# The dense layer of a tile group in the round of its own items, ten groups instead of nine, and a bias of three bf16 rows

## The reference

```python
neigh_sum = segment_sum(ln(x)[src], dst, num_segments=6250)      # 100000 edges, sorted by dst
deg = segment_sum(ones, dst, num_segments=6250)
h = concatenate([ln(x), neigh_sum / maximum(deg, 1.0)[:, None]], axis=-1)
out = relu(h @ W + b)                                            # 512 -> 256
x = x + out / maximum(norm(out, axis=-1), 1e-12)
gate_scores = ln(x) @ Wg.T + bg                                  # 8 experts, top 2 of each node
...
```

## Time and profile before

| what | us |
|---|---|
| median of three runs (lowest, highest) | 3768.05 (3767.71, 3769.46) |
| profiled execution: its time, and its span | 3773.36, 3771.6 |
| mean granted TensorE clock | 0.869 |
| TensorE, VectorE, ScalarE, GpSimd busy | 2839.5, 1832.5, 963.7, 1716.8 |
| gather stage of layer 0: first indirect load | 104.5 |
| last indirect load, end of the stage | 1107.9, 1263.7 |

### The profile page before, as it was taken

One profiled execution on the slowest core, in us unless ns is written; L12 is line 12 of the kernel. 1 busy time (PEld: TensorE's weight loads), 2 busy tenths in 40 slices (PEclk: granted clock), 3 DMA queues, 4 the chain that ended last, 5 costly groups with the idle time before them and its releaser, 6 DMA issues. The chain is left out here.

```text
span 3771.6 us, 56373 instructions
## 1 busy us (share of the span) xinstructions
PE 2839.5 (75%) x13227; PEld 2325.9 (62%) x13228; DVE 1832.5 (49%) x4097; ACT 963.7 (26%) x3408; POOL 1716.8 (46%) x1811
## 2 busy tenths in 40 slices
PE   1566778778877599999998536767667667738999
PEld 0355657656655388888887425555555455538998
DVE  5322333444566411111111847878788888773444
ACT  0000100100111122222222323433344344315544
POOL 0677777777740122222222067667666666300000
PEclk9888988889887699999999768888888888857999
DMA  5333333333320121222221633333333333200000
GB/s 171 92 104 105 105 104 115 114 104 111 115 73 15 68 84 57 107 70 94 85 81 31 195 110 107 98 100 104 101 101 101 101 99 98 59 17 7 21 19 21
DMA packets 152075, 326.67 MB, mean 87 GB/s; under 512 B 38677, under 2 KB 89837, under 8 KB 147870
## 3 DMA queue, kind: packets, MB, share of 16 engines
q0 software_dynamic: 85824, 236.38, 22.0%
q1 hardware_dynamic: 59758, 83.04, 6.6%
q10 hardware_dynamic: 6416, 6.42, 0.5%
HBM read 286.41 MB, written 41.40 MB: 87 GB/s over the span
## 5 line engine op out<-in xcount | busy, mean ns | idle before, releaser
L633 POOL DMA_INDIRECT G<-g_rows,srcT x784 | 745.2, 951 | 435.2 <-issue 243.3
L633 POOL DMA_INDIRECT G<-h_rows,srcT x784 | 747.4, 953 | 270.2 <-issue 236.6
L814 PE MATMUL pS<-G,O 128*128 x2336 | 593.1, 418 | 208.4 <-SPq L801 182.5
L814 PEld LDWEIGHTS pS<-G,O 128*128 128x128 f32 x2336 | 487.6, 211 | 312.1 <-issue 228.6
L1713 PE MATMUL pS<-G,O 128*128 x2336 | 637.4, 436 | 56.3 <-DVE O L1861 56.3
L1713 PEld LDWEIGHTS pS<-G,O 128*128 128x128 f32 x2336 | 491.6, 214 | 195.4 <-issue 79.7
L1341 PE MATMUL pH<-XT,w1s 128*128 128x256 f32 x1728 | 384.6, 381 | 1.4 <-SPq L1312 1.4
L1351 PE MATMUL pY<-w2s,HE 128*128 128x256 f32 x1728 | 381.9, 379 | 0.0
L1341 PEld LDWEIGHTS pH<-XT,w1s 128*128 128x128 f32 x1728 | 330.2, 191 | 47.2 <-issue 1.8
L1366 ACT ACTIVATE HE<-pH,b1s 128x256 f32<-128x256 f32 x432 | 204.9, 474 | 584.1 <-PE pH L1341 584.1
L1351 PEld LDWEIGHTS pY<-w2s,HE 128*128 128x128 f32 x1728 | 324.1, 190 | 41.8
(11 more groups left out here) (294 smaller groups left out, 3526.9 us busy)
## 6 DMA issues: line engine op xcount, KB each, us to landing
w1s<-in_W_dram SPq DMA_DIRECT2D x16, 1024.0 KB, 5.0
w2s<-in_W_dram SPq DMA_DIRECT2D x16, 1024.0 KB, 7.6
G<-h_rows,srcT POOLq DMA_INDIRECT x784, 2.8
Y<-y_rows SPq DMA_DIRECT2D x49, 256.0 KB, 4.4
G<-g_rows,srcT POOLq DMA_INDIRECT x784, 2.8
g_rows<-OUT SPq DMA_DIRECT2D x49, 132.0 KB, 2.3
h_rows<-ACC SPq DMA_DIRECT2D x7, 896.0 KB, 5.4
X<-in_x_dram SPq DMA_DIRECT2D x1, 6144.0 KB
```

The lines of the kernel that those rows point to most:

```text
L633: pool.indirect_dma_start(out=G[:, c % (ring * Q), 0:width], out_offset=None, in_=rows, in_offset=bass.IndirectOffsetOnAxis(ap=srcT[:, c:c ...
L814: mm = nc.tensor.matmul(pS[k][:, 0:W], O[:, k, q, :], G[:, bass.ds((s % R0) * Q + q, 1), :].rearrange("p a d -> p (a d)"), start=(q == 0), ...
```

## The change

1. Group r's dense layer runs in round r, right behind its items, instead of in round r + 1. All the other steps of a group move up by one round too (LAGS = 3).
2. The groups are (7, 7, 7, 6, 5, 5, 4, 3, 3, 2).
3. VectorE prepares the first two tiles of a group (tile_in) ahead of choose, and rdeg is a small buffer reused by each group.
4. The elementwise output of the square goes to an SBUF tile sq instead of pO, and dense and turn_h1 wait for the relu (s_relu) and no longer for the square (s_sq).
5. The bias is loaded to three partitions, split at the start into three bf16 rows whose sum is the float32 value (ten VectorE instructions), and added by one bf16 matmul of three rows of ones, instead of a float32 matmul of one row. TensorE and ScalarE wait for the split once (s_b3).

```diff
         self.R0 = 7
-        self.GROUPS = (7, 7, 7, 7, 7, 6, 4, 2, 2)
+        self.GROUPS = (7, 7, 7, 6, 5, 5, 4, 3, 3, 2)
         self.ECOLS = self.NT + self.NT % 2
...
         LCOLS = NE * z.ECOLS
-        LAGS = 4
+        LAGS = 3
 
...
             W0 = sb("W0", [P, 2 * KD, D])
-            b0 = sb("b0", [1, D])
+            b3 = sb("b3", [3, D], BF16)
+            ones_b = sb("ones_b", [3, P], BF16)
+            sq = sb("sq", [P, D])
             Wg = sb("Wg", [P, KD, NE])
...
             HT1 = sb("HT1", [P, 2, D])
-            rdeg = sb("rdeg", [P, NT])
+            rdeg = sb("rdeg", [P, GMAX])
             ssq = sb("ssq", [P, NT])
...
             s_list = sem("s_list3")
+            s_b3 = sem("s_b33")
             s_dve = sem("s_dve0")
...
                     sp.dma_start(W0[:], a["W0"].rearrange("(k p) n -> p k n", p=P)).then_inc(s_w, 16)
-                    sp.dma_start(b0[:], a["b0"].unsqueeze(0)).then_inc(s_w, 16)
+                    sp.dma_start(HT[0:3, 0, 0:D], a["b0"].unsqueeze(0).to_broadcast([3, D])).then_inc(s_w, 16)
                     sp.dma_start(Wg[:], a["WgT"].rearrange("(k p) n -> p k n", p=P)).then_inc(s_w, 16)
...
                         if t:
-                            pe.wait_ge(s_sq, t)
+                            pe.wait_ge(s_relu, t)
                         for m in range(2 * KD):
...
                                              start=(m == 0), stop=False)
-                        nc.tensor.matmul(pO[:, 0:D], ones[0:1, :], b0[:], start=False, stop=True).then_inc(s_out, 1)
+                        nc.tensor.matmul(pO[:, 0:D], ones_b[:], b3[:], start=False, stop=True).then_inc(s_out, 1)
 
...
                         pe.wait_ge(s_ht, dense_done)
-                        pe.wait_ge(s_sq, dense_done)
+                        pe.wait_ge(s_relu, dense_done)
                         if t >= 2:
...
                     pe.wait_ge(s_w, 64)
+                    pe.wait_ge(s_b3, 1)
                     for r in range(NG + LAGS):
                         if r < NG:
-                            if r > 3:
-                                pe.wait_ge(s_rankread, r - 3)
+                            if r > 2:
+                                pe.wait_ge(s_rankread, r - 2)
                             items(r)
-                        new, old = tiles_of(r - 1), tiles_of(r - 4)
-                        h1_done = FIRST[max(r - 2, 0)] if r - 2 <= NG else NT
+                        new, old = tiles_of(r), tiles_of(r - 3)
+                        h1_done = FIRST[max(r - 1, 0)] if r - 1 <= NG else NT
                         if new:
...
                                 to_lists(old[n])
-                        if 0 <= r - 3 < NG:
-                            ranks(r - 3, r)
-                        mid = tiles_of(r - 2)
-                        dense_done = FIRST[min(r, NG)]
+                        if 0 <= r - 2 < NG:
+                            ranks(r - 2, r)
+                        mid = tiles_of(r - 1)
+                        dense_done = FIRST[min(r + 1, NG)]
                         if mid:
...
                                     turn_h1(t + 1, dense_done)
-                                gate(t, r - 2)
+                                gate(t, r - 1)
 
...
                             act.wait_ge(s_sq, t)
-                        nc.scalar.activation(pO[:, 0:D], ACC[:, t, 0:D], ACT.Square, accum_out=ssq[:, t:t + 1]).then_inc(s_sq, 1)
+                        nc.scalar.activation(sq[:], ACC[:, t, 0:D], ACT.Square, accum_out=ssq[:, t:t + 1]).then_inc(s_sq, 1)
 
...
 
-                    for r in range(1, NG + 2):
-                        new = tiles_of(r - 1)
+                    act.wait_ge(s_b3, 2)
+                    for r in range(NG + 1):
+                        new = tiles_of(r)
                         if new:
                             turned_in(new[0])
-                        mid = tiles_of(r - 2)
+                        mid = tiles_of(r - 1)
                         var_at = min(-(-len(mid) // 2), len(new)) if mid else -1
...
                             if n == var_at:
-                                var_root(r - 2)
+                                var_root(r - 1)
                             if t + 1 in new:
...
                         if var_at == len(new):
-                            var_root(r - 2)
+                            var_root(r - 1)
                         if new:
...
                         if mid:
-                            act.wait_ge(s_h1, FIRST[r - 1])
-                            act.dma_start(h1_rows[FIRST[r - 2] * P:FIRST[r - 1] * P, :].rearrange("(t p) d -> p t d", p=P),
-                                          ACC[:, FIRST[r - 2]:FIRST[r - 1], 0:D]).then_inc(s_h1st, 16)
+                            act.wait_ge(s_h1, FIRST[r])
+                            act.dma_start(h1_rows[FIRST[r - 1] * P:FIRST[r] * P, :].rearrange("(t p) d -> p t d", p=P),
+                                          ACC[:, FIRST[r - 1]:FIRST[r], 0:D]).then_inc(s_h1st, 16)
                     act.wait_ge(s_h1st, 16 * NG)
...
                     dve.wait_ge(s_w, 64)
+                    bias, rest1, rest2 = HT[0:3, 0, 0:D], HT[0:3, 1, 0:D], HT[0:3, 1, D:2 * D]
+                    part = [B1[0:3, m, c, 0:D] for m, c in ((0, 0), (0, 1), (1, 0))]
+                    loc.link(nc.vector.memset(ones_b[:], 1.0))
+                    loc.link(nc.vector.tensor_copy(part[0], bias))
+                    loc.link(nc.vector.tensor_tensor(rest1, bias, part[0], ALU.subtract))
+                    loc.link(nc.vector.tensor_copy(part[1], rest1))
+                    loc.link(nc.vector.tensor_tensor(rest2, rest1, part[1], ALU.subtract))
+                    loc.link(nc.vector.tensor_copy(part[2], rest2))
+                    loc.link(nc.vector.tensor_scalar(b3[:], part[0], ident[0:3, 0:1], None, ALU.mult))
+                    for n in (1, 2):
+                        loc.link(nc.vector.scalar_tensor_tensor(out=b3[:], in0=part[n], scalar=ident[0:3, n:n + 1],
+                                                                in1=b3[:], op0=ALU.mult, op1=ALU.add))
+                    dve.sem_inc(s_b3, 2)
 
...
 
-                    def tile_in(t):
+                    def tile_in(t, n):
                         if t >= 2:
...
                         ln_apply(IN[:, t % 2], X[:, t, :], slice(t, t + 1)).then_inc(s_in, 1)
-                        nc.vector.tensor_scalar(ACC[:, t, 0:D], ACC[:, t, 0:D], rdeg[:, t:t + 1], None, ALU.mult)\
+                        nc.vector.tensor_scalar(ACC[:, t, 0:D], ACC[:, t, 0:D], rdeg[:, n:n + 1], None, ALU.mult)\
                             .then_inc(s_in, 1)
...
                             items(r)
-                        if 0 <= r - 3 < NG:
-                            choose(r - 3)
-                        new, mid, old = tiles_of(r - 1), tiles_of(r - 2), tiles_of(r - 4)
+                        new, mid, old = tiles_of(r), tiles_of(r - 1), tiles_of(r - 3)
                         if new:
-                            v = slice(new[0], new[-1] + 1)
-                            loc.link(nc.vector.tensor_scalar(rdeg[:, v], ACC[:, v, D], 1.0, None, ALU.max))
+                            v = slice(0, len(new))
+                            loc.link(nc.vector.tensor_scalar(rdeg[:, v], ACC[:, new[0]:new[-1] + 1, D], 1.0, None, ALU.max))
                             loc.link(nc.vector.reciprocal(rdeg[:, v], rdeg[:, v]))
+                            tile_in(new[0], 0)
+                            tile_in(new[1], 1)
+                        if 0 <= r - 2 < NG:
+                            choose(r - 2)
                         if mid:
                             v = slice(mid[0], mid[-1] + 1)
-                            dve.wait_ge(s_root0, r - 1)
+                            dve.wait_ge(s_root0, r)
                             loc.link(nc.vector.tensor_scalar(rnorm[:, v], rnorm[:, v], NORM_EPS, None, ALU.max))
...
                         for n in range(max(len(new), steps, len(old))):
-                            if n < len(new):
-                                tile_in(new[n])
+                            if 2 <= n < len(new):
+                                tile_in(new[n], n)
                             for t in mid[2 * n:2 * n + 2]:
...
                             if n < len(old):
-                                list_hots(old[n], r - 4)
+                                list_hots(old[n], r - 3)
                             for t in mid[2 * n:2 * n + 2]:
...
                         if mid:
-                            dve.wait_ge(s_vroot, r - 1)
+                            dve.wait_ge(s_vroot, r)
                             ln_group_rstd(loc, mid[0], mid[-1] + 1)
...
                                 ln_apply(ACC[:, t, 0:D], X[:, t, :], slice(t, t + 1)).then_inc(s_h1, 1)
-                        if 0 <= r - 3 < NG:
-                            positions(r - 3)
+                        if 0 <= r - 2 < NG:
+                            positions(r - 2)
```

## The result

| | kernel before | changed kernel |
|---|---|---|
| median (lowest to highest), us | 3768.73 (3767.71 to 3769.46) | 3722.97 (3721.76 to 3724.19) |
| ratio, 95% interval | | 0.9879 (0.9862 to 0.9896) |
| profiled span, us | 3771.6 | 3721.9 |
| end of the first gather stage, us | 1264.7 | 1184.2 |
| second gather stage: first to last indirect load, us | 2184.2 to 3257.0 | 2103.0 to 3209.1 |

Faster, but the time lies 9 us above the forecast range. The end of a stage is told here by the first instruction of the next one on GpSimd; it comes about 1 us behind the last work of the stage, 1263.7, that the prediction used. The first gather stage (of layer 0) gained 80.5 us; 33 of these were lost again in the second gather stage (of the attention layer), whose code the change doesn't touch. The spans of the two profiled executions lie 49.7 us apart, the medians 45.8.

The account below looks back on a forecast made before the run. GpSimd's gather bounds layer 0's stage until tile 41, then a VectorE and TensorE chain; 949.6 + 138 + 101.2 = 1188.8 ends it 74.9 us sooner. Profiled 3773.4 − 74.9 = 3698.5, median 3693, range 3679 to 3714.

Parts of the forecast that it names:

- its sum: Layer 0's gather stage ends at 949.6 + 138 + 101.2 = 1188.8, 74.9 us sooner; later stages only shift.
- Group work: VectorE's rounds 6 to 12 behind tile 41, apart from items: 138 us, against 209.5 before.
- Waits: VectorE's waits in group work behind tile 41: 5 us each in rounds 6 to 8, 19 in all.
- the formula: VectorE's own time per round, without waits, from counts of new, mid, list and choose tiles; 119.0 us behind tile 41.
- Items: The same 22 items, 16 matmuls each, in three phases behind tile 41: 101.2 us again, bounds 92 and 112.
- Reaching tile 41: First gather stage, paced by the gather until tile 41 is complete: 949.6 us, 0 to 15 late as bound.
- rival C: Tile 41 is reached 15 us late because the added round isn't hidden: gain 60, 3708 us; 7%.
- Ring: GpSimd's gather in the first stage: loads end near 1088 us without the 15 us stall for a ring slot.
- Bias: TensorE's bias pass in the dense layer: 0.14 us as one bf16 pass, instead of 0.63.
- Start: Splitting the bias on VectorE at the start: ten instructions, at most 10 × 0.5 us, costing nothing.
- Rival D: TensorE stays at the lower clock in the whole tail of the first gather stage: 3778 us, slower; 2%.
- Rival A: Waits behind tile 41 stay at 7.3 us in each of four rounds: gain 62, 3706 us; 18%.

Follow-up runs that it names:

- e7: Changed kernel with 40 idle memsets, the square written to pO again and dense and turn_h1 waiting for it: 3691.2 us.
- e9: Changed kernel with 40 idle memsets, the two tile_in of a group again behind choose: 3683.7 us (0.9775).
- e15: Changed kernel with 40 idle memsets, tile_in ahead of choose, run again for side-by-side comparison: 3692.5 us (0.9795).
- e16: Changed kernel with 40 idle memsets, the two tile_in behind choose, run again side by side with e15: 3690.5 us (0.9784).
- e12: Changed kernel with 20 idle VectorE memsets ahead of the second gather's loop: 3690.1 us.
- e17: Kernel before with 66 idle VectorE memsets ahead of the second gather's loop: 3805.9 us.
- e1: Kernel before with 84 idle VectorE memsets ahead of the second gather's loop, as many instructions as the change adds: 3800.7 us (1.0093).
- e13: Changed kernel with 120 idle VectorE memsets ahead of the second gather's loop: 3713.6 us.

## Why the prediction was wrong, step by step

- **The step that failed** is in its sum: "All later stages start behind the stage's end and shift with it". They start behind it, but the second gather stage also became 33 us longer (1106.1 for 1072.8 us). I had counted the instructions added on VectorE only by their time, and not by what the 84 added ones do to the place of the code behind them; the change of the later stages stood at nothing, without a reason. With the loop moved away, the same change measures 3687.8 to 3693.0: the forecast was 3693. The first stage itself gained 80.5 us for 74.9.
- **Group work**: forecast 138, measured 138.6. By rounds: 31.1, 27.9 and 26.4 forecast for rounds 6 to 8, 30.3, 28.0 and 27.2 measured; rounds 9 to 12 52.6 and 53.1.
- **Waits**: group work less the formula leaves 4.2, 5.1 and 5.8 us in rounds 6 to 8 and 4.5 in rounds 9 to 12, 19.6 in all; 5 a round and 19 in all were forecast. The reason was at least half wrong: neither the square (e7) nor the earlier tile_in (e9, e15, e16) shortened them by anything that shows. That they fell with the list tiles, of which fewer stand in each round, is my reading; no run changes these alone.
- **Items**: forecast 101.2, measured 92.4, the lower bound. The 22 items at 3.44 us each are 75.7 in both kernels; a phase adds 5.6 us instead of the 8.5 that I took. The lines below show why in the last phase: before, TensorE's gate matmuls ran to 1153.98, 3.5 us past VectorE's end of the group work (1150.5), and the 6.0 us to the first item matmul held this rest. Now they end at 1110.3, ahead of VectorE's end (1110.8), and the first item matmul starts 2.0 us behind it. The two phases ahead went the same way: the first item matmul came 5.0 and 4.5 us behind VectorE's end before, and 2.8 and 2.4 after. The three together make 8.3 of the 8.8 us. The term was mis-sized by 9 us; that it was one figure of a place with leftover work, and not the price of a phase, is what I missed.

TensorE at the end of the group work ahead of the last item phase, before:

```profile
1152.27 1.71 PE L873 MATMUL pZ<-Wg,HT 128*128 128x8 f32 x8
```

and after:

```profile
1109.07 1.25 PE L876 MATMUL pZ<-Wg,HT 128*128 128x8 f32 x8
1112.80 16.72 PE L817 MATMUL pS<-G,O 128*128 x64 [2.48 <-issue]
```

- **Reaching tile 41**: forecast 949.6, measured 952.3, and 948 to 956 over the runs; rival C (15 us late) did not come.
- **Ring**: the wait of 15.46 us went (1.2 in all), loads end at 1091.1 (forecast 1088).
- **Bias**: 0.21 us for 0.14, nothing in the end.
- **Start**: the split took 106.9 to 110.0 on VectorE, hidden before the first item (123.0 against 122.6).
- **Rival D** (low clock): didn't come; clocks are 0.80 to 0.92 down to the last stretch, 0.71. Rival A (waits stay at 7.3) would have given 151 us of group work, and 138.6 were measured; that its 3706 is nearer to the result than my value is an accident.
- **The range** held bounds for every term of the first stage and none for the later ones; I had named "if later stages change by more than a few us" as what would prove me wrong, and gave it no share.
- **The strip**: GpSimd is busy in slices 2 to 12 of the kernel before, not 2 to 13, and 13 is the empty one. No number of the forecast was taken from it.

## What to carry to other kernels

A change that adds or removes instructions moves every loop behind it in the instruction memory. Here a hardware loop of VectorE of 288 instructions costs 3 us more at each branch back where it reaches into a fourth stretch of 128, so an edit ahead of it moves the total by some 33 us of either sign. By the same reading, which no run tests with another loop, one of up to 257 instructions has no such place. Look at the first instruction behind each long loop's backward branch: `issue` of some 3 us there, and more packets on the instruction queue, say that it has happened, and some idle instructions ahead take it away (20 were enough in e12). Judge an edit by the length of the stage that it touches, with the loops behind it held in place, before judging by the total.

## What was unexpected about the hardware

- The stall: 2.8 to 3.6 us at a backward branch (up to 4.4 in e17), ten times, with five more instruction packets of 8.2 KB each time (e1: 63 for 13 from 2190 to 3200 us); at one place a second wait of 2.1 to 2.5 us ahead of the loop's fourth instruction.
- It comes when the loop reaches into a fourth stretch of 128 instructions, and it is all or nothing: the second gather's loads take 1072 to 1074 us without it in thirteen traces (1065.7 in one), 1104.9 to 1109.0 with it in four (1094.0 in one, 1117.9 with two waits).
- 28.7 us more of waits on VectorE, which is busy for some 0.78 of the stage, cost 33.3 us of the stage: nothing covered them. In e13 26.9 us more cost 21.2, which stays open.
- The three-row bf16 pass of 256 columns took 0.21 us to the next start, a third of the two float32 passes of one row (0.63).
